# Two chained linear maps in the first layer of a two-layer kernel, done in the other order on one Trainium2 core

## The reference, cut to what matters

```python
# 32 samples, x is (32, 128, 2048)
# first layer
att   = softmax(mlp(cond))                        # (32, 8)
agg_w = einsum('bk,koi->boi', att, weight)        # one 128x128 matrix per sample
agg_b = att @ bias_k                              # (32, 128)
y     = einsum('boi,bih->boh', agg_w, x) + agg_b[:, :, None]
W_eff = W + sum_e coeffs[e] * scales[e] * Bf[e] @ A[e]     # 2048 x 2048, low-rank part folded in
x1    = x + y @ W_eff.T + bias
# second layer: grouped convolution of x1, a feed-forward net with GELU, added to x1
```

## Time and profile before

| what | us |
|---|---|
| median of 3 runs (2637.3 to 2639.1) | 2639.07 |
| the profiled execution | 2640.44 |
| span of its trace | 2638.5 |
| granted TensorE clock, mean | 0.991 of full speed |
| TensorE matmul busy | 2570.8 (97%) |
| VectorE busy | 1837.5 (70%) |
| ScalarE busy | 1001.5 (38%) |
| GpSimd busy | 955.3 (36%) |

### The profile page before, as it was taken

How to read it: one execution, slowest core, us unless ns; L and a number is a source line. 1 busy time by engine, 2 the same in 40 slices (tenths; PEclk the granted TensorE clock), 3 DMA queues, 4 the chain that set the end, 5 groups by cost and what they waited for, 6 DMA issues and landing times. The chain is left out here.

```text
span 2638.5 us, 39106 instructions
## 1 busy us (share of the span) xinstructions
PE 2570.8 (97%) x12090; PEld 2111.6 (80%) x12090; DVE 1837.5 (70%) x2671; ACT 1001.5 (38%) x1631; POOL 955.3 (36%) x826
## 2 busy tenths in 40 slices
PE   7899999999999999999999999999999999999997
PEld 6678888888888888888888778888888888888775
DVE  6555555865555855567444668888888888888776
ACT  3211211322122322233222455555555555555563
POOL 2265654556553554332232312222222222222231
PEclk9999999999999999999999999999999999999998
DMA  8845554755544776576455664576767676767687
GB/s 306 310 168 184 195 174 152 266 170 200 190 156 169 244 226 215 172 239 208 156 167 182 196 178 130 158 219 205 230 206 222 210 223 203 231 212 223 192 272 246
DMA packets 417283, 541.04 MB, mean 205 GB/s; under 512 B 36248, under 2 KB 270064, under 8 KB 417072
## 3 DMA queue, kind: packets, MB, share of 16 engines
q1 hardware_dynamic: 315584, 307.40, 38.9%
q10 hardware_dynamic: 77376, 154.27, 15.6%
q0 software_dynamic: 24112, 76.80, 9.3%
HBM read 309.72 MB, written 228.61 MB: 204 GB/s over the span
## 5 line engine op out<-in xcount | busy, mean ns | idle before, releaser
L427 PE MATMUL ps_c<-w_hi,ring_hi 128*128 128x512 f32 x1792 | 714.1, 398 | 9.6 <-DVE ring_lo L910 5.2
L427 PE MATMUL ps_c<-w_hi,ring_lo 128*128 128x512 f32 x1792 | 708.6, 395 | 0.0
L427 PE MATMUL ps_c<-w_lo,ring_hi 128*128 128x512 f32 x1792 | 708.3, 395 | 0.0
L574 ACT ACTIVATE ring_hi<-raw_n 128x512 fp32r<-128x512 f32 x384 | 241.2, 631 | 901.6 <-DVE raw_n L871 247.3
L1290 POOL DMA_INDIRECT y_d<-y_s,idx x128 | 147.2, 1150 | 736.3 <-ACT y_s L1458 688.0
L427 PEld LDWEIGHTS ps_c<-w_hi,ring_hi 128*128 128x128 f32 x1792 | 338.7, 189 | 87.1 <-DVE ring_lo L910 10.2
L1425 ACT ACTIVATE kern<-ps_up 128x512 f32<-128x512 f32 x512 | 306.2, 598 | 260.3 <-PE ps_up L1308 235.4
L427 PEld LDWEIGHTS ps_c<-w_hi,ring_lo 128*128 128x128 f32 x1792 | 338.4, 189 | 79.2
L427 PEld LDWEIGHTS ps_c<-w_lo,ring_hi 128*128 128x128 f32 x1792 | 338.8, 189 | 76.4
L1542 DVE TENSOR_TENSOR g_lo<-kern,g_hi 128x512 fp32r<-128x512 f32 x512 | 354.7, 693 | 41.0 <-ACT g_hi L1429 20.6
L931 DVE TENSOR_TENSOR r_early<-ps_c,r_early 128x512 f32<-128x512 f32 x256 | 176.8, 691 | 284.3 <-PE ps_c L427 284.3
(11 more groups left out here) (199 smaller groups left out, 3843.5 us busy)
## 6 DMA issues: line engine op xcount, KB each, us to landing
u_d<-raw_n ACTq DMA_DIRECT2D x64, 512.0 KB, 3.3
x_d<-r_early ACTq DMA_DIRECT2D x128, 256.0 KB, 3.4
x_d<-x_s ACTq DMA_DIRECT2D x128, 256.0 KB, 2.6
raw_n<-u_d SPq DMA_DIRECT2D x64, 512.0 KB, 3.7
u_s<-x_d SPq DMA_DIRECT2D x496, 64.0 KB, 2.7
z_d<-x_s SPq DMA_DIRECT2D x120, 256.0 KB
rear<-y_d SPq DMA_DIRECT2D x112, 256.0 KB
rear<-x_d SPq DMA_DIRECT2D x112, 256.0 KB
```

The costliest lines, as they stand in the source:

```text
L427: mm = nc.tensor.matmul(bank, a[:, dc, :], w[k][:, dc, :], start=(first and dc == 0 and n == 0), stop=(dc == 3 and n == 2), skip_group_che ...
L574: nc.scalar.activation(ring_hi[g % RING][:].rearrange("p a n -> p (a n)"), ring_raw[p][k], ACT.Copy).then_inc(hi_ready, 1)
```

## The change

Products now take x itself, transposed on the host into `x_t`. No matrix is applied in the first 16 quads; in the last 16, each of the eight finished 128 x 512 pieces of a quad is split into halves `v_hi`, `v_lo`, multiplied by the sample's mixed matrix (split into `agg_hi`, `agg_lo`) in three matmuls, `mix_v`, and added to a residual. The residual x + bias is made by VectorE in quads 0 to 15 (`add_bias`), stored as `xb_d`, loaded again in quads 16 to 31, where ScalarE makes `agg_b * rowsum(W)` and GpSimd adds it (`add_e`). Sums of W over rows are gathered by GpSimd (`sums`), then summed over partitions by a matmul with ones (`sum_rows`, twice). The ring is of four buffers and the halves are made three items ahead, and stand first in each slot. In the first 16 quads the take of k = 0, 2, 3, 5 is a plain copy. Other edits: tiles of the opening share rooms sooner; the experts are mixed in quad 0; 16 instead of 24 weight chunks are split during quad 31 and 16 in the lead, with GpSimd in VectorE's place and SyncE's queue in GpSimd's; the walk has nine slots after the last item (`TRAIL`).

```diff
-EARLY = 24
+FINAL = QUADS // 2
+EARLY = 16
-RING = 6
+RING = 4
+TRAIL = 9
+MIX_SLOT = (6, 8, 11, 12, 14, 15, 16, 18)
+BIAS_SLOT = (1, 2, 4, 6, 8, 9, 11, 13)
@@ room(tile)
-    return (tuple(range(10)) + tuple(range(10)) + (2, 3, 4, 5, 0, 8, 1, 9, 2, 3, 4, 5))[tile]
+    return (tuple(range(10)) + (0, 1, 2, 3, 4, 5, 6, 9, 0, 1) + (2, 3, 7, 1, 2, 3, 7, 1, 3, 0, 6, 1))[tile]
@@ TensorE
-            def make_u(q, j):
...
-                for dc in range(8):
-                    mm = nc.tensor.matmul(ps_v[:, n % 2, dc * P:(dc + 1) * P], x_s[j][:, dc * P:(dc + 1) * P],
-                                          agg[:, j, :], start=True, stop=True)
+            def mix_v(n):
...
+                pe.wait_ge(vlo_ready, i + 1)
+                wait(pe, mixed, i - 3)
...
+                for a, v in ((agg_hi, v_hi), (agg_hi, v_lo), (agg_lo, v_hi)):
+                    mm = nc.tensor.matmul(ps_w[n % 4], a[:, j, :], v[n % 2][:], start=(a is agg_hi and v is v_hi),
+                                          stop=(a is agg_lo))
+                mm.then_inc(mix_mm, 1)
+            def sum_rows(half):
...
+                for n in range(2):
+                    mm = nc.tensor.matmul(ps_w[n], ones[:].to_broadcast([P, P]), sums[half][:, n * 512:(n + 1) * 512],
+                                          start=True, stop=True)
@@ ScalarE, a slot: split(ahead) now stands before load_tw and split_tw
+                ahead = product_from(q, t, 3)
+                if ahead and ahead != (0, 0):
+                    split(*ahead)
+                for n in mixed_at(*divmod(ITEMS * q + t + 1, ITEMS)):
+                    split_v(n)
...
+                for n in mixed_at(q, t):
+                    add_bias_of_mix(n)
@@ GpSimd
-            def residual(q, p, blk):
-                nc.gpsimd.tensor_tensor(r_s[p][blk], x_s[j][:, here], bias_s[:, here], ALU.add).then_inc(r_set, 1)
+            def add_e(n):
+                pool.wait_ge(res_in[n % 4], 16 * (n // 4 + 1))
+                pool.wait_ge(e_ready, n - 8 * FINAL + 1)
+                nc.gpsimd.tensor_tensor(res[n % 4], res[n % 4], e, ALU.add).then_inc(res_set, 1)
@@ GpSimd, mix_piece: two sums ahead of the four differences
+                sum_piece(pool, nc.gpsimd, q, c)
@@ GpSimd, a slot
+                if mixes(q) and t in (2, 9):
+                    mix_piece(q, t // 9)
+                for n in mixed_at(*divmod(ITEMS * q + t - 1, ITEMS)):
+                    add_e(n)
...
+                for n in freed_chunks(q, t):
+                    split_early(n)
@@ VectorE
-            def take_u(q, j):
-                nc.vector.tensor_tensor(raw[j].rearrange("p (c o) -> p c o", o=P),
-                                        ps_v[:, n % 2, :].rearrange("p (c o) -> p c o", o=P),
-                                        bc[:, j, :].unsqueeze(1).to_broadcast([P, 8, P]), ALU.add).then_inc(u_ready, 1)
+            def split_v(n):
+                nc.vector.tensor_tensor(v_lo[n % 2][:], r_s[p][blk], fp32(v_hi[n % 2][:]), ALU.subtract).then_inc(vlo_ready, 1)
+            def take_mixed(n):
+                dve.wait_ge(mix_mm, i + 1)
+                dve.wait_ge(res_set, n + 1)
+                nc.vector.tensor_tensor(res[n % 4], ps_w[n % 4], res[n % 4], ALU.add).then_inc(mixed, 1)
+            def add_bias(n):
+                nc.vector.tensor_tensor(res[n % 4], res[n % 4], bias_s[:, sub * 512:(sub + 1) * 512], ALU.add).then_inc(res_set, 1)
@@ SyncE, layer 1
+            def load_weights(n):
+                sp.wait_ge(wsplit_lo, G + max(n - 3, EARLY))
+                sp.dma_start(stage[n % 4], weight_chunk(up, down, n)).then_inc(w_in[n % 4], 16)
@@ GpSimd, layer 1, in the lead (was VectorE's)
+            def split_weights(n):
+                pool.wait_ge(wsplit_hi, G + n + 1)
+                nc.gpsimd.tensor_tensor(chunk(w_lo, n), stage[n % 4], fp32(chunk(w_hi, n)),
+                                        ALU.subtract).then_inc(wsplit_lo, 1)
```

More of the change, by code:

```diff
@@ L326, in load_mix @@
[L326 to L336 removed]
+                if t in (22, 24, 26, 28):
+                    load_raw(0, {22: 0, 24: 2, 26: 1, 28: 3}[t])
@@ L789, in slot @@
[L789 to L800 removed]
+                    if t in (10, 11):
+                        sum1(q + 1, t - 10)
@@ L802, in _ @@
+            quads(slot, -4)
         @block.vector
```

732 lines of the change are left out of this document (385 added, 347 removed).

## The result

| | before | changed |
|---|---|---|
| median of the runs | 2639.09 us (2637.3 to 2642.4) | 2671.25 us (2667.6 to 2673.9) |
| span of the profiled execution | 2638.5 us | 2672.1 us |
| ratio of the times, 95% interval | | 1.0119 (1.0102 to 1.0137) |

A forecast was written before the change was run, and what follows sets the result against it. TensorE's work, with its waits and slow stretches, was taken as the bound. Terms -21.1 - 17.8 + 3 + 1 + 15.4 + 1 + 6 + 1.2 = -11.3 us gave 2628 us, range 2607 to 2652.

The forecast's parts named there:

- 1, TensorE's work: All quads: 113.9 us of `make_u` removed, 89.2 us of piece matmuls and 3.6 of row sums added, net -21.1 us.
- 2 and 3, quad 0 and the opening: Quad 0's waits and slow matmuls go, -17.8 us; late tiles in the opening +3, quad 0's sums of quarters +1.
- 4, the changes of W: VectorE falls behind at quads 8, 16 and 24: 3.5, 3.5 and 10 us, less 1.6 lost before, +15.4 us.
- 12 if half do: Change of W from quad 23: VectorE 12 us behind if half of GpSimd's operations hit it, 17 if all.
- 5, quads 17 to 20: `take_mixed` waits 4 to 5 us for GpSimd's mixing, under the cover of three items: +1 us, 0 to +20.
- 6, the end of layer 0: After the last product: later last result +2.5, GpSimd's weight subtractions before the last `add_e` +3.5, together +6 us.
- 7, the lead: Layer 1's lead: GpSimd's two chunks a step hold up the next load, +1.2 us, 0 to +6.
- Cost at nothing: Plain first-half copies, loads and stores of x + bias, ScalarE's `split_v` and `agg_b * rowsum`: free under idle time.
- (a): Rival: VectorE becomes the bound in the second half, slower, about 2655 us; chance 0.20.
- (b): Rival: VectorE's lag is absorbed, changes of W cost 3 instead of 17 us, total about 2612; chance 0.17.
- (c): Rival: opening gains nothing, late tiles cost 10 us, quad 0's waits partly return (5), about 2640; chance 0.16.

The follow-up runs named there:

- run 3: Changed kernel with each of VectorE's 84 subtractions for the low parts of W touching 2 of 512 columns: 2645.25 us.
- run 4: Changed kernel with the first half's 8 copies a quad from PSUM moved from VectorE to ScalarE: 2661.51 us.
- run 5: Changed kernel with the low parts of W at each change spread over 18 items instead of 14: 2662.44 us.
- run 6: Changed kernel with GpSimd's 128 additions of the row-sum term to res touching 2 of 512 columns: 2647.76 us.
- run 1: Changed kernel without nearly all of the row sums that GpSimd makes in quads 17 to 20: 2652.01 us.
- run 2: Changed kernel with all 24 pieces of mixed W and row sums moved to quads 1 to 7 and 9 to 13: 2662.3 us.
- run 8: Changed kernel with the first 16 splits of layer 1's weights cut to 2 of 512 columns on ScalarE and GpSimd: 2667.66 us.
- version 14: Changed kernel with edits like run 2, run 4, run 5 and run 9, lead reworked, early low parts on VectorE, memset in quad 25: 2634.23 us, ratio 0.9979.
- run 9: Changed kernel with the last two res pieces loaded into two rooms of their own: 2667.03 us.
- run 11: Changed kernel with 24 early chunks of layer 1's weights instead of 16, and 8 in the lead: 2674.76 us.
- run 10: Changed kernel's lead: loads back on GpSimd 2676.12 us; also low parts on VectorE 2674.26; low parts alone 2669.05; that with one chunk a step 2664.39.
- run 7: version 14 before its early low parts and memset moved (2636.71 us), with 7 of 28 low-part subtractions per change of W on GpSimd: 2641.85 us.

## Why the prediction was wrong, point by point

- **1, TensorE's work: right.** 38.95 and 44.5 us a plain quad for 39.04 and 44.6. At the start of quad 16 all of the gain and more was there.
- **2 and 3, quad 0 and the opening: right.** Quad 0 starts at 116.56, near 115, and its only listed wait on TensorE is 0.64 us. By its end 27.2 us are won. My terms with the eight `make_u` of that stretch (14.2 us) come to 28.0. Some of the closeness is luck: in the 17 other kernels the same stretch wins 23.3 to 27.4 us.
- **4, the changes of W: right in kind, too small.** 8.9, 8.2 and 11.4 us for 3.5, 3.5 and 10, so 26.9 instead of 15.4 after the 1.6 lost before. The mis-sized terms are quads 8 and 16. I counted VectorE 8 us behind at each and took most of it as covered, as it was in quad 16 before, and next to nothing was. The price of 1.1 us for a GpSimd operation was right. The ring has four rooms now where it had six, so the halves run three items ahead where they ran four; that this is why nothing was left over is argued, no run changes the ring. Run 3 shows that at quad 8 it is VectorE's low parts of W (7.6 us), run 4 that 5.5 us less of VectorE's work a quad bring 2.9 us back at least. At quad 16 run 3 takes away 3.8 us and runs 4, 5 and 6 nothing beyond the spread, so half of that loss stays open. At quads 23 and 24 the count was near (its "12 if half do" halves only the eight new operations; with all sixteen halved it is 8): run 6 takes away half of the loss, run 3 two thirds.
- **5, quads 17 to 20: the step that failed most.** "4 to 5 us, under the cover of three items" was the wait of one piece, and the trace has such waits, 4.37 us and seven more of 2.8 to 4.4. What failed is the overlap: they come in four quads in a row, twice in each, while `v_lo` takes up to 1.78 us in place of 0.68 beside the same GpSimd operations, and TensorE waits seven times, 12.6 us by the list. 16.4 us instead of 1; runs 1 and 2 take 15.3 and 16.4 of them away in two ways, run 6 four fifths of them in a third.
- **6, the end of layer 0: right in kind, too small.** 14.9 us instead of 8.8 (6 and the 2.8 of part 1). The early splits, which I priced at 3.5 us, cost 1.7 to 3.8 (run 8), and version 14 gives back 2.6 by taking GpSimd's share out. The rest of the gap, 11.3 us above before, is the chain of the last four pieces: high half, low half beside a GpSimd operation (1.2 to 1.8 us), product at half clock (0.43 us a step), addition. I had given it 2.5 us and the 2.8 of the products. Run 9 shows that the loads are not in it. Which link weighs most I have not tried.
- **7, the lead: wrong.** 8.9 us instead of 1.2. I looked only at GpSimd's subtractions, and these cost 2.6 us at most. Some 4 to 6 come with the eight chunks more (run 11), which I had given nothing but a later load. Of these 3.3 to 3.8 come back when the chunks are loaded one a step and not in SP's queue, and neither alone does it (run 10). SP's queue, where a load is issued for 0.42 to 0.46 us, I had not counted at all.
- **Cost at nothing:** ScalarE's new work was rightly free, even with 8 copies more a quad. For the loads of x + bias there is one listed wait of note, GpSimd's 2.30 us at the end, and run 9 shows that it cost nothing.
- **The rivals.** (a) happened as its test had it (quads 17 to 20 over 46 us), but by the waits of GpSimd's queue and not by the price of 1.1 us an operation alone: in quads 25 to 30, with 16 to 18 GpSimd operations each, no wait of TensorE is listed. Runs 3, 6 and 7 show the price itself: `w_lo` and `v_lo`, with two SBUF inputs, go from 0.68 to 1.0 to 1.8 us beside GpSimd, and even one of 2 columns to 1.25 us, while all 576 operations that read PSUM (L1006, L1013, L1031) stay at 0.67 to 0.69. The rule of the Trainium skill (SBUF — State Buffer, Who interferes with whom) says that the two exclude each other for a whole instruction. The trace agrees. (b) and (c) are out: nothing was absorbed, and the opening gave its gain. Even (a)'s 2655 us was 16 us too fast. Its own terms, 19 us more in quads 17 to 20 and 12 at the changes of W on top of 2628, come to 2659, and I never added up the rivals' losses with those of the two ends.

## What to carry to other kernels

A change that moves work from the bound engine to its feeders has to be added up at each place where a feeder was already full: here TensorE's gain was as computed and was given back at six places. Look at what stands in front of a waiting instruction in the queue of each engine it waits for, and how often in a row; and move such background work to stretches where its engine's neighbour is idle, which here cost no more than a table of quads. Count GpSimd's work twice, once for itself and once for what it adds to VectorE's SBUF-to-SBUF operations beside it, here up to 1.1 us for each one met.
